# Expert tiles of a mixture-of-experts layer: the gathered rows turned by moves within SBUF and VectorE instead of by TensorE

## The reference

```
xn  = layernorm(x)                                   # 4096 x 256
att = causal attention with 16 heads of 16, kernel taylor_exp(q).taylor_exp(k), projected by Wo
logits = xn @ Wg                                     # 8 experts, the 2 largest per token, softmax of the two
h = xn @ W1[e]; g = xn @ W2[e]                       # 256 -> 512
y = (silu(h) * g) @ W3[e]                            # 512 -> 256
out = x + att + sum over a token's two experts of gate * y
```

## Time and profile before

| | |
|---|---|
| median of 3 runs | 646.82 us (646.73 to 647.78) |
| the profiled execution | 645.7 us, of which the span from first to last instruction is 644.0 |
| PE / DVE / ACT / POOL busy over the span | 96% / 70% / 54% / 56% |
| mean granted TensorE clock | 0.988 of full |
| expert stage | from about 308 us to the end |

### The profile page before, as it was taken

One profiled execution on the slowest core, in us unless ns is written; L12 is line 12 of the kernel. 1 busy time (PEld: TensorE's weight loads), 2 busy tenths in 40 slices (PEclk: granted clock), 3 DMA queues, 4 the chain that ended last, 5 costly groups with the idle time before them and its releaser, 6 DMA issues.

```text
span 644.0 us, 16648 instructions
## 1 busy us (share of the span) xinstructions
PE 617.4 (96%) x5170; PEld 475.2 (74%) x5170; DVE 450.4 (70%) x1134; ACT 348.4 (54%) x515; POOL 358.4 (56%) x453
## 2 busy tenths in 40 slices
PE   7899999999999999989999899999999999999994
PEld 6655666656666666655788788888888888888884
DVE  5776878788787766687787467666666666666663
ACT  3477878787887777676564333333333333333331
POOL 4147463636465554647247466665666666666644
PEclk8799999999999999999999999999999999999998
DMA  4553454555644434544864456666666666666543
GB/s 131 149 120 116 105 133 113 152 142 135 157 96 122 99 124 84 153 106 146 280 198 69 101 113 122 121 123 124 121 123 126 116 125 126 117 126 121 121 93 43
DMA packets 73348, 80.37 MB, mean 125 GB/s; under 512 B 12369, under 2 KB 61393, under 8 KB 73265
## 3 DMA queue, kind: packets, MB, share of 16 engines
q1 hardware_dynamic: 56000, 50.51, 30.4%
q0 software_dynamic: 16704, 28.12, 23.0%
q10 hardware_dynamic: 560, 0.66, 0.3%
HBM read 27.72 MB, written 22.95 MB: 79 GB/s over the span
## 4 chain that ended last, share of the span: by engine, by line
PE 44%; issue 25%; POOL 17%; DVE 4%; DMA 3%; ACT 3%; POOLq 2%; SPq 1%; ACTq 0%; DVEq 0%
PE banks L1164 10%; PE banks L1146 8%; POOL xg L539 8%; PE banks L1184 8%; POOL out L565 6%; PE banks L1290 4%; PE banks L1193 4%; PE banks L1228 3%; POOL mark L551 2%; POOLq L549 2%; PE banks L1311 2%; PE banks L1213 1%; ACT T L603 1%; PE banks L1219 1%; DMA K<-Kt 1%
## 5 line engine op out<-in xcount | busy, mean ns | idle before, releaser
L565 POOL DMA_INDIRECT out<-yo,xw x71 | 112.6, 1586 | 103.4 <-DVE yo L1093 82.7
L530 POOL TENSOR_SCALAR_AFFINE_SELECT T<-T 128x512 f32<-128x512 f32 x128 | 80.4, 639 | 110.3 <-ACT T L609 45.3
L1290 PE MATMUL banks<-w12h,xgh 128*128 x284 | 112.7, 397 | 2.9 <-DVE xgl L1071 2.8
L1290 PE MATMUL banks<-w12l,xgh 128*128 x284 | 111.4, 392 | 0.0
L1290 PE MATMUL banks<-w12h,xgl 128*128 x284 | 111.0, 391 | 0.0
L1105 DVE TENSOR_TENSOR hs<-banks,hs 128x512 f32<-128x512 f32 x71 | 49.1, 692 | 84.8 <-PE banks L1290 79.9
L700 ACT ACTIVATE sTh<-banks 128x512 fp32r<-128x512 f32 x71 | 42.3, 597 | 91.8 <-DVE banks L1081 74.6
L539 POOL DMA_INDIRECT xg<-xs_scr,glist x71 | 71.5, 1007 | 24.5 <-issue 20.3
L1164 PE MATMUL banks<-T,vau 128*17 128x512 f32 (+3 forms) x1024 | 75.6, 434 | 1.0 <-POOL T L530 1.0
L521 POOL DMA_INDIRECT xs_scr<-xb,slots x64 | 64.1, 1002 | 20.2 <-issue 12.6
L1146 PE MATMUL banks<-Q,K 32*128 32x256 f32 (+2 forms) x1024 | 71.4, 362 | 3.5 <-DMA K<-Kt 2.4
(11 more groups left out here) (186 smaller groups left out, 1245.2 us busy)
## 6 DMA issues: line engine op xcount, KB each, us to landing
hq<-hs SPq DMA_DIRECT2D x244, 64.0 KB
Q<-Q SPq DMA_DIRECT2D x128, 64.0 KB, 2.4
w12r<-w SPq DMA_DIRECT2D x16, 512.0 KB, 4.7
out<-xa SPq DMA_DIRECT2D x16, 256.0 KB
w3r<-w SPq DMA_DIRECT2D x8, 512.0 KB, 8.3
K<-Kt SPq DMA_DIRECT2D x124, 32.0 KB
xa<-x SPq DMA_DIRECT2D x7, 512.0 KB, 4.5
xg<-xs_scr,glist POOLq DMA_INDIRECT x71
```

The costliest lines, as they stand in the source:

```text
L530: e.affine_select(out=v, in_=v, pattern=[[0, 4], [1, P]], compare_op=ALU.is_ge, fill=-1.0, base=0, channel_multiplier=-1).then_inc(s["g_mk ...
L565: e.indirect_dma_start(out, bass.IndirectOffsetOnAxis(xw[:, t % XR, NE:NE + 1].bitcast(U32), 0), yo[:, t % 2, :], None, compute_op=ALU.add ...
L1290: i = e.matmul(banks[:, 2 * (t % 2) + m, :], a[:, k, :], w[:, bass.ds(expert[t] * 4 + (2 * k + m), 1), :], start=(k == 0 and n == 0), stop ...
```

## The change

It is in how x of a gathered tile gets from rows to columns, for tiles XS = 12 to 70; tiles 0 to 11 keep the transposes on PE.

- `move_x(t)`: four DMAs of 32 KB carry `xg[:, t % GR, 64r : 64r + 64]` (128 partitions, 256 bytes each) to 32 partitions of `xq[t % 2]` (1024 bytes each). SP issues r = 0, 1 of tile t + 4 behind `move_h(t)`; ACT issues r = 2, 3 of tile t + 3 behind `expert_x(t + 1)`. Each waits for the gather and for the transpose that last read that half of `xq`.
- `turn_x(t)`: a stream transpose by DVE of `xq[t % 2]` into bank 4, in iteration t - 2 behind `expert_x`. `transpose_g(t + 1)` goes from PE's loop for t + 1 >= 12.
- To make the order of columns fit, `w12` is laid out on the host with contraction index 2p + k instead of 128k + p, PE's transposes read even and odd columns, and `xgh` and `xgl` are written with a stride.
- The ring `xg` has 3 slots instead of 4, and `gather(t)` waits for all four moves of tile t - 3 (`x_moved`) instead of for PE. POOL's step t issues gathers up to t + 9 instead of t + 7 (t + 4 instead of t + 5 before tile 8).
- The gate copy is a function of its own, `weights`, and runs in iteration t up to tile t + 3 instead of t + 1 from tile 12 on. It copies 9 words instead of 16.
- `up` waits for `xgh` at its start and for `xgl` only at its third matmul.

```diff
-GR = 4
+GR = 3
+XS = 12
@@ helpers
+        def move_x(e, t, some):
+            e.wait_ge(s[f"d_g{t % GR}"], 16 * (t // GR + 1))
+            if t >= XS + 2:
+                e.wait_ge(s["v_tx"], t - XS - 1)
+            for r in some:
+                e.dma_start(xq[t % 2][32 * r:32 * r + 32, :],
+                            xg[:, t % GR, 64 * r:64 * r + 64]).then_inc(s[f"d_xq{t % 2}"], 16)
+
+        def x_moved(e, t):
+            e.wait_ge(s[f"d_xq{t % 2}"], 64 * ((t - XS) // 2 + 1))
@@ sync_program
             for t in range(TS, TE):
                 move_h(t)
+                if XS <= t + 4 < NT:
+                    move_x(e, t + 4, range(2))
@@ gpsimd_program
             def gather(t):
                 if t >= GR:
                     e.wait_ge(s["v_xw"], t - GR + 1)
-                    e.wait_ge(s["p_gt"], t - GR + 1)
+                    if t - GR < XS:
+                        e.wait_ge(s["p_gt"], t - GR + 1)
+                    else:
+                        x_moved(e, t - GR)
...
-                upto = t + 4 if t == 0 else t + 5 if t < TS else t + 7
+                upto = t + 3 if t == 0 else t + 4 if t < TS else t + 9
@@ scalar_program
             def expert_x(t):
-                e.wait_ge(s["p_gt"], t + 1)
+                if t < XS:
+                    e.wait_ge(s["p_gt"], t + 1)
+                else:
+                    e.wait_ge(s["v_tx"], t - XS + 1)
...
                 if t + 1 < NT:
                     expert_x(t + 1)
+                if XS <= t + 3 < NT:
+                    move_x(e, t + 3, range(2, 4))
@@ vector_program
+            def turn_x(t):
+                x_moved(e, t)
+                e.wait_ge(s["v_gt"], t)
+                e.transpose(banks[:, 4, 0:256], xq[t % 2].rearrange("p (t c k) -> p t k c", t=4, k=2)).then_inc(s["v_tx"], 1)
+
+            def weights(t):
                 e.wait_ge(s[f"d_g{t % GR}"], 16 * (t // GR + 1))
                 if t >= XR:
                     e.wait_ge(s[f"d_sc{t % 2}"], 16 * ((t - XR) // 2 + 1))
-                e.tensor_copy(xw[:, t % XR, :], xg[:, t % GR, D:XW]).then_inc(s["v_xw"], 1)
+                e.tensor_copy(xw[:, t % XR, :], xg[:, t % GR, D:D + WI]).then_inc(s["v_xw"], 1)
...
                 if t + 1 < NT:
                     expert_x(t + 1)
+                if XS <= t + 2 < NT:
+                    turn_x(t + 2)
+                while weighed < min(t + 3 if t + 3 >= XS else t + 1, NT - 1):
+                    weighed += 1
+                    weights(weighed)
@@ tensor_program
             def up(t, m):
-                e.wait_ge(s["v_gt"], t + 1)
+                e.wait_ge(s["a_gt"], t + 1)
...
                     for n, (a, w) in enumerate(((xgh, W12h), (xgh, W12l), (xgl, W12h))):
+                        if k == 0 and n == 2:
+                            e.wait_ge(s["v_gt"], t + 1)
...
-                if t + 1 < NT:
+                if t + 1 < XS:
                     transpose_g(t + 1)
```

More of the change, by code:

```diff
@@ L22 @@
 XW = D + NE + 8
+WI = NE + 1
 VW = D + NE
@@ L175, in build @@
         xgl = rx.take("xgl", 256, F32R, (2, P))
-        xw = rx.take("xw", XR * 16, F32, (XR, 16))
+        xq = [rm.take("xq0", D), rx.take("xq1", D)]
+        xw = rx.take("xw", XR * WI, F32, (XR, WI))
         held = rx.take("held", 72, I32)
@@ L292, in build @@
                 "a_si", "v_mu", "p_st", "a_st", "v_st", "p_yo", "v_yo", "d_sc0", "d_sc1",
-                "c_hold", "v_hold", "g_hold", "d_hq0", "d_hq1", "v_th")
+                "c_hold", "v_hold", "g_hold", "d_hq0", "d_hq1", "v_th",
+                "d_xq0", "d_xq1", "v_tx")
         MISC, USED = misc_uses()
@@ L333, in s_turned, with x_bank, x_turned @@
             return v.rearrange("p (k c t) -> p k c t", k=4, t=4) if TS <= t < TE else v
+        def x_bank(t):
+            v = banks[:, 4, 0:256]
+            return v.rearrange("p (t k c) -> p k c t", t=4, k=2) if t >= XS else v.rearrange("p (k n) -> p k n", k=2)
+        def x_turned(tile, t):
+            return tile.rearrange("p k (c t) -> p k c t", t=4) if t >= XS else tile[:]
+        def move_x(e, t, some):
[7 more added lines that the diff above has]
+            e.wait_ge(s[f"d_xq{t % 2}"], 64 * ((t - XS) // 2 + 1))
         def x_landed(e, b):
@@ L685, in expert_x @@
             def expert_x(t):
-                e.wait_ge(s["p_gt"], t + 1)
+                if t < XS:
+                    e.wait_ge(s["p_gt"], t + 1)
+                else:
+                    e.wait_ge(s["v_tx"], t - XS + 1)
                 if t:
                     e.wait_ge(s["p_g"], t)
-                e.activation(xgh[:], banks[:, 4, 0:256].rearrange("p (k n) -> p k n", k=2), ACT.Copy).then_inc(s["a_gt"], 1)
+                e.activation(x_turned(xgh, t), x_bank(t), ACT.Copy).then_inc(s["a_gt"], 1)
             def high_s(t):
@@ L1070, in expert_x @@
                 e.wait_ge(s["a_gt"], t + 1)
-                e.tensor_tensor(xgl[:], banks[:, 4, 0:256].rearrange("p (k n) -> p k n", k=2), xgh[:].bitcast(F32),
-                                ALU.subtract).then_inc(s["v_gt"], 1)
+                e.tensor_tensor(x_turned(xgl, t), x_bank(t), x_turned(xgh, t).bitcast(F32), ALU.subtract).then_inc(s["v_gt"], 1)
+            def turn_x(t):
[3 more added lines that the diff above has]
+            def weights(t):
                 e.wait_ge(s[f"d_g{t % GR}"], 16 * (t // GR + 1))
@@ L1096, in vector_program @@
             expert_x(0)
+            weights(0)
             step("y", LAST, 1)
@@ L1099, in vector_program @@
             step("o", LAST, 0)
+            weighed = 0
             for t in range(NT):
@@ L1277, in transpose_g @@
                     e.wait_ge(s["v_gt"], t)
+                pairs = xg[:, t % GR, 0:D].rearrange("p (n k) -> p k n", k=2)
                 for k in range(2):
-                    i = e.transpose(banks[:, 4, k * P:(k + 1) * P], xg[:, t % GR, k * P:(k + 1) * P], ident[:])
+                    i = e.transpose(banks[:, 4, k * P:(k + 1) * P], pairs[:, k, :], ident[:])
                 i.then_inc(s["p_gt"], 1)
@@ L1380 @@
         "wo": rows(wo),
-        "w12": w12.reshape(NE, 2, P, 2, HID).transpose(2, 0, 1, 3, 4).reshape(P, NE * 4, HID),
+        "w12": w12.reshape(NE, P, 2, 2, HID).transpose(1, 0, 2, 3, 4).reshape(P, NE * 4, HID),
         "w3": np.asarray(L0_ffn_W3).reshape(NE, 4, 4, 32, D).transpose(1, 3, 0, 2, 4).reshape(P, NE * 4, D),
```

## The result

The changed kernel takes 661.12 us in the median of 4 runs (656.05 to 662.03), the kernel before 646.78 on the same chips: ratio 1.022, 95% interval 1.018 to 1.026. It is slower by 14 us. That lies outside the stated range of 634 to 655 and on the other side of the forecast.

The account below looks back on a forecast made before the run. PE was taken to bound the kernel before at 4.40 us a tile, then the new ring at 4.38: 59 tiles give 1.2 us, edges 1.5, together 2.7, so 644.1 us; forecast 640 to 647, 8-in-10 range 634 to 655.

Parts of the forecast that it names:

- PE: Expert stage: without the two transposes of xg a tile loses 0.20 us of PE, 4.40 to 4.20; at most 11.8 us.
- DVE, ACT, DMA, each by itself: Added loads per tile: turn_x 0.42 us on DVE, two issues of 1.3 us on ACT, both hidden; DMA 11 or 22 points.
- the rival with 0.04: DMA engines fill up if a 256 B packet costs twice a 512 B one: 4.71 us a tile, 665 us; chance 0.04.
- The ring: Gate copy, turn_s, SP's issues, x landing, gather, scatter, back three tiles on: lap 13.15 us, 4.38 a tile.
- the ring makes it slower: Same ring with SP's stalls counted in full or landings delayed: at a 13.5 us lap 4.50 a tile, 653 us; chance 0.29.
- All other terms are hidden on paper: Argument for PE staying the bound: PE has no gap, and everything else the change adds is covered.
- first rival: PE stays the bound at 4.20 us a tile: 635 us, up to 640; chance 0.27.
- The edges: One-time effects outside the steady tiles: 1.5 and 2 us gained, 2 lost where gathered tiles switch paths; net gain 1.5 us.
- the split wait's 2 us: At up's start, waiting for xgh alone: four waits like 1.06 us become about 0.5, together 2 us gained.
- The hand-over: gather(12) lands some 3 us later, at 363, delaying SP, ACT and DVE: 0 to 4 us of PE lost, 2 taken.
- The 1.5 us that a late ring was to eat first: Slack used up before PE loses: 0.85 us of DVE idle time and some 0.6 us of later xgl, gained once.
- a measurement tells 0.2%: What a measurement of this kernel can tell from no change: about 0.2%, 1.3 us.

Follow-up runs that it names:

- e7_both: Changed kernel with gathers up to t + 8 and turn_s ahead of turn_x and the gate copies on DVE; 640.43 us, 0.992 of the kernel before.
- e10_no_moves: e7_both without the x moves and their waits from tile 14 on (old rows are turned); 631.13 us, 0.978 of the kernel before.
- e3_smallx: Changed kernel with each x move from tile 14 on carrying 32 packets of 256 B instead of 128; 660.05 us, 1.025 of the kernel before.
- e1_gather8: Changed kernel with POOL issuing gathers up to t + 8 instead of t + 9; 646.06 us, 1.001 of the kernel before.
- e4_pool: Changed kernel with three more small POOL operations between gather and scatter of tiles 9 to 62; 675.27 us, 1.047 of the kernel before.
- e6_turn_s_first: Changed kernel with only turn_s put ahead of turn_x and the gate copies on DVE; 648.00 us, 1.003 of the kernel before.
- e8_five_three: e7_both with one of SP's two x moves given to ACT; 639.44 us, 0.992 of the kernel before.
- e5_split: Kernel before with only the split wait: up waits for xgh first, for xgl at its third matmul; 640.49 us, 0.993; repeated, 0.997.
- e11_one_wait: e7_both with up waiting for xgl at its start again; 644.69 us, 0.999 of the kernel before.
- e9_small_x: e8_five_three with each x move from tile 14 on carrying 32 packets of 256 B instead of 128; 634.55 us, 0.986 of the kernel before.

## Why the prediction was wrong

*PE*: right. No transpose of xg after tile 11; `down` takes 1.41 (1.44 was read), and a tile of e7_both without a wait 4.14. So there are about 0.25 us a tile to win, not 0.20; e10_no_moves wins them, and is 14.5 us faster than the kernel before with the split wait in it.

*DVE, ACT, DMA, each by itself*: `turn_x` takes 0.46 (0.42 taken). ACT's issues take 0.61 in the median and are hidden, even three. That the DMA engines fill up was the rival with 0.04: e3_smallx refutes it for the changed kernel. Its premise, that a packet of 256 B costs twice one of 512 B, can be read off the trace of the changed kernel, where ACT's x moves have a queue of their own; the row of the queues from 500 to 540 us, against the earlier trace rows:

```profile
q10 hardware_dynamic: 2592, 0.59, 7.1%
```

7.1% of 16 x 40 us over 2592 packets is 17.5 ns a packet, where queue 1 took 22.2% for 5314, 26.7 ns, before (packets of 4 B that carry no data are counted in both). A packet of half the bytes takes two thirds of the time, not twice it.

*The ring*: right in its form, place and consequence, shown by e1_gather8 and e4_pool, and it is the rival "the ring makes it slower" that came true. The step that failed is its size, 13.15 us taken and 14.08 measured: "The stalls do not all count [...] I take 13.15". Means over the 44 laps that begin in iterations 18 to 61 of the changed kernel, from its trace:

| leg | predicted | measured |
|---|---|---|
| gate copy to SP's first issue | 0.92 | 1.13 |
| six issues | 3.73 (4.18 with stalls) | 4.10 |
| last issue's end to the gather | 2.5 | 2.95 |
| gather to scatter | 1.76 | 1.56 |
| scatter to gate copy | 4.1 | 4.34 (4.15 in the 20 laps where the copy waited for it) |
| lap | 13.15 taken, 12.5 to 13.9 | 14.08 |

Three errors of the same sort. I priced each leg by its undisturbed row and then let part of the stalls be worked off; the six issues take 4.10 in the mean, so nearly all of the stalls counted (3.73 without any, 4.18 with all). For the landing of x, with half the bytes, I took a little less than that of hq; it is 0.37 longer, and e3_smallx shows that bytes give back only 0.24. And in 18 of the 44 laps SP was still busy with the last round when `turn_s` ended, so that its first issue came 0.31 us behind `turn_s` in the mean, 0.07 before: a queue filled to 4.1 of 4.7 us hands on its own stalls. The scatter's landing was priced right: where the gate copy waited for it, it took 4.15. In the other 24 laps DVE itself came late, for which the hq lap of e1_gather8 is a likely reason; no run separates it. At the measured lap the rule of the slower rival (59 x (4.69 - 4.40)) gives 17 us, 664.

*"All other terms are hidden on paper"*, in the first rival: wrong too. I had put `turn_x` ahead of `turn_s`, saw that SP would start 0.42 later, and did not follow that around: the lap from product to product could have been summed from rows of before: 1.91 + 0.42 to SP's first issue, 2.48 of issues, 2.58 to SiLU, 0.60 for SiLU, 7.99 us for two tiles or 4.00 each. That would have shown how little reserve there is under 4.20, though not the 4.46 of e1_gather8, to which late issues and landings are added. Had the ring been absent, the kernel would still have gained nothing (e1_gather8).

*The edges*: the split wait's 2 us are in the range of what was measured. The hand-over, tiles 8 to 14, takes 27.5 us against 26.2 before: 1.3 more, within my 0 to 4. It looks as foreseen; SP's timeline:

```profile
356.57 2.61 SPq L467 DMA_DIRECT2D hq<-hs  x4
363.11 1.19 SPq L351 DMA_DIRECT2D xq<-xg  x2
364.35 2.62 SPq L467 DMA_DIRECT2D hq<-hs  x4
```

The moves of tile 12 wait for its gather until 363.11 (363 was estimated), with hq of tile 9 behind them. The 1.5 us that a late ring was to eat first are not to be seen: tiles 13 and 14 already take 5.33 and 5.06 us.

The Trainium skill's fit of 2.0 us and the bytes ("DMA: Bandwidth & Descriptors", Anatomy of one DMA), an estimate of 2.1 us for an x move, is below the trace: 2.95 us from the end of its issue to the gather. The page gives the fit for a queue in software, and x moves go by hardware queues.

What the change's parts are worth, tiles 12 to 65 (53 tiles), from the products' spacing: 0.24 us a tile in PE's work (4.41 to 4.17, 12.8 us); given back 0.16 to what the moves cost with both laps cut (4.17 to 4.33), 0.13 to the hq lap (4.33 to 4.46), and 0.23 to the ring (4.46 to 4.69). The last two shares hold in this order only: e6_turn_s_first, the order on DVE alone, takes off 0.19. The forecast also held that a measurement tells 0.2%; the kernel before ranges from 641 to 649 us within one group, and the intervals are 0.2% to 0.6% to either side. The versions that beat the kernel before, e7_both and e8_five_three, do it by 0.8%; e5_split alone does it by 0.3% to 0.7%. e7_both and e5_split, of one group, are even at 640.4 and 640.5 us, and e11_one_wait, which has the moved x with both laps cut but not the split wait, is even with the kernel before (0.999). So no run shows a gain from the moved x itself; what e7_both gains can all come from the split wait.

## What to carry to other kernels

When a change adds a wait to a queue that issues work for others, write down who is behind it and follow the chain until it comes back: the lap over the number of tiles it spans is a bound on the period, beside that of the busiest engine, and no engine's busy share shows it. Price a lap by means, stalls included, and count a queue as a resource like an engine. In a program with several rings the order in which two independent instructions stand on one engine (a gather before a scatter, `turn_x` before `turn_s`) can be worth more than the work that was taken away.

## What the runs showed of the hardware that I had not expected

An issue on SP takes 0.60 us in the median, and now and then one takes far longer. Between 380 and 620 us the kernel before has ten of 0.9 us or more (1.2 to 2.0 long), the changed kernel 13 (0.9 to 1.8), 16 to 19 us apart but for one step of 35. Six issues came to 4.10 us in the mean.

Now and then both readers of a semaphore of PE start late. In e8_five_three, the timeline of PE and ACT and DVE at one such place:

```profile
518.86 0.39 PE L1338 MATMUL banks<-w12h,xgl 128*128 x1
...
519.35 0.69 DVE L1145 TENSOR_TENSOR hs<-banks,hs 128x512 f32<-128x512 f32 x1 [0.76 <-PE banks L1338]
...
523.00 0.39 PE L1338 MATMUL banks<-w12h,xgl 128*128 x1
523.22 0.63 PE L1359 MATMUL banks<-w3h,sTh 128*128 x4
...
525.03 0.38 ACT L719 ACTIVATE xgh<-banks 128x256 fp32r<-128x256 f32 x1 [1.83 <-remote]
525.04 0.69 DVE L1145 TENSOR_TENSOR hs<-banks,hs 128x512 f32<-128x512 f32 x1 [1.61 <-remote]
```

The product normally starts 0.5 us after the start of the last `up` matmul; here it starts 2.04 after, ACT's copy of xgh at the same moment, while PE had gone on. Places like it (0.9 us or more, with SiLU done 0.4 us or more before) stand six times in tiles 12 to 64 of e8_five_three, twice in e7_both and three times in e9_small_x, with the DMA engines at 79%, 78% and 70%, and never in the kernel before at 63%. They do not follow that share alone, as the changed kernel has none at 71%; what holds the semaphore back is open.
